# A gate bias matmul over 9 rows instead of 128, and four setup steps of VectorE in another order

## The chip, the core and the metric

The program runs on one core of a Trainium2 chip. A core has TensorE (PE: matmuls, with the weight load PEld as a row of its own), VectorE (DVE), ScalarE (ACT), GpSimd (POOL) and SyncE (SP), whose queue starts DMAs. Each engine runs its own list of instructions in order, and the lists meet only at semaphores: an instruction counts one up, another engine waits for a count. The metric is the device time in microseconds (us) of one execution, the median of three runs.

## The reference

Four layers on an activation of shape (16, 512, 256), each followed by a layer norm; cut to what is computed:

```python
x = layernorm(x + attention(x))            # 16 query heads, one key/value head of 16
x = layernorm(x + ternary_ffn(x))          # weights round(w/mean|w|) clipped to -1, 0, 1; gelu
x = layernorm(x + ssm_and_cfc(x))
x = layernorm(x + mx_quantised_linear(x))  # FP6 blocks of 32

def ssm_and_cfc(x):                        # S = 512 time steps, in order
    xn = layernorm(x) * norm_g + norm_b
    B_all = xn @ B_w.T + B_b
    states = A_pow * cumsum(B_all / max(A_pow, 1e-8))
    ssm_out = states @ C_w.T + C_b
    def step(h, xt):
        cat = [xt, h]
        ff1 = tanh(cat @ ff1_w.T + ff1_b); ff2 = tanh(cat @ ff2_w.T + ff2_b)
        t = sigmoid((cat @ ta_w.T + ta_b) * 0.1 + (cat @ tb_w.T + tb_b))
        return ff1 * (1 - t) + t * ff2
    return x + scan(step, ssm_out) @ out_w.T + out_b
```

The input-side biases of the three gates (`ff1`, `ff2`, `t`) are one number for each of 128 hidden units and each gate. The kernel adds them with a matmul, and that matmul is the one that changes.

## The kernel before, in words

The work is cut into 64 tiles of 128 rows (4 batch items by 32 positions). A tile passes through stages that run in different turns of one loop (`tile_time`, 16 ticks of 4 slots a turn): queries, row maxima of the scores, attention, feed-forward, state scan, 8 recurrence steps, last layer. The tables `PE_AT`, `ACT_AT`, `DVE_AT` and `POOL_AT` say at which slot of a turn each engine does its part, so the order on each engine is fixed by hand. After the loop a tail does the recurrence steps that are left.

**The bias matmul.** `input_bias` (L740) opens the sum in PSUM for the 8 recurrence steps of a tile: 384 columns (8 steps, 3 gates, 16 batch items). Its stationary operand `bias_rows` has 9 meaningful rows, three bf16 pieces for each of three gates; its moving operand `gate_of` has ones in the row of its own gate. In the kernel before both have 128 partitions, the other 119 filled with zeros, which GpSimd writes (L1484 to L1493). In the loop it is issued once a turn at slot 4 (`INPUT=4`), between a score matmul (L698) and the six matmuls of the gates' state part (L746); in the tail five times more.

**The array's tiles.** A matmul is built with a part of the 128 by 128 array that it uses. L698, L740 and L746 use all of it. L730, L762 and L619 use 128 rows by 32 columns, four such beside one another. L560 and L562 use 64 rows by 128 columns each, and run as a pair.

**The setup.** Before the loop all engines run steps `b` = 0 to 18 that turn weights, make keys and values, and from `b` = 11 on take the row maxima of tile 0. PE issues a pair of score matmuls (`max_pair`, L560 and L562); DVE reduces it (`take_maxima`, L1122); PE waits for each reduction (`max_taken`) before the next pair. Between them DVE has `setup_part(b)`: at `b` = 11 the scale of the second ternary weight (L1157 to L1159), for which GpSimd waits to compare the weight with it (L1517), at 12 the ternary weight (L1162), which waits for GpSimd, at 14 the additions of the biases (L1190, L1191), which wait for PE's products with vectors (L665, L668, at `b` = 13). At 15 `order_queries` copies tile 1's queries (L1136, L1138). At `b` = 12 and 16 DVE also splits keys (`split_keys`, L1219 to L1225), ahead of all this.

Of the kernel before, what the change touches and what calls it, by code (L numbers as in the profile page):

```python
# [8 lines left out]
ACT = mybir.ActivationFunctionType  # L9
AX_X = mybir.AxisListType.X  # L10
F32 = mybir.dt.float32
BF16 = mybir.dt.bfloat16
FP8 = mybir.dt.float8e4

P = 128
BLOCK_POS = 32
GROUP = P // BLOCK_POS
TICKS = 16
SLOTS = 4 * TICKS
STEPS = 8  # L20
# [22 lines left out]
def block_net(nc, x, w_q, w_k, w_v, w_out, softmax_scale, W1, b1, W2, b2, A_log, B_w, B_b, C_w, C_b,  # L43
              norm_g, norm_b, ff1_w, ff1_b, ff2_w, ff2_b, ta_w, ta_b, tb_w, tb_b, out_w, out_b,
              ffn_w, ffn_bias, q_dram, m_dram, x2_dram, out):
    B, S, D = x.shape
# [56 lines left out]
    def wait(eng, sem, count):  # L103

        if count > 0:
            eng.wait_ge(sem, count)

    def settle(eng):

        eng.sem_inc(settled[eng.engine], 1)

    with ExitStack() as ctx:
        def sb(name, shape, dt=F32):
            return ctx.enter_context(nc.sbuf_tensor(name, shape, dt))

        def sem(name):
            return ctx.enter_context(nc.semaphore(name))

        def bank(name):  # L120
            return ctx.enter_context(nc.psum_tensor(name, [P, 512], F32))
# [6 lines left out]
        gate_bank = bank("gate_bank")  # L128
# [29 lines left out]
        bias_piece = sb("bias_piece", [P, 3, 3])  # L158
        bias_rest = sb("bias_rest", [P, 2, 3])
        bias_bf = sb("bias_bf", [P, 2, 3], BF16)  # L160
        bias_rows = sb("bias_rows", [P, P], BF16)
        gate_ones = sb("gate_ones", [P, STEPS, 3, B])
        gate_of = sb("gate_of", [P, STEPS, 3, B], BF16)
        apow = sb("apow", [P, S])
        ainv = sb("ainv", [P, S])
        small = sb("small", [P, 32])
# [86 lines left out]
        gate_made = sem("gate_made")  # L253
# [10 lines left out]
        bias_rows_made = sem("bias_rows_made")  # L264
# [114 lines left out]
        FIRST_MAX = 11  # L379
# [166 lines left out]
        def _(pe):  # L546
# [137 lines left out]
                max_pair(0, pair)  # L684
            pe.wait_ge(v_kept, R)
            pe.wait_ge(bias_rows_made, 1)
            pe.wait_ge(gate_made, 5)

            def tile_time(c, r, n):
                for t in range(TICKS):  # L690
# [236 lines left out]
        def _(act):  # L927
# [14 lines left out]
            def copy_x(m):  # L942
                act.wait_ge(filled[1], use(1, "XT", m) + 1)
                if m > 0:
                    act.wait_ge(filled[1], use(1, "Q", m - 1) + 1)
                act.activation(xTq[:, :, :], gen_bank[1][:, 0:D].rearrange("p (k t) -> p k t", k=KT), ACT.Copy).then_inc(emptied[1], 1)

            def first_piece(m):
                act.wait_ge(filled[1], use(1, "Q", m) + 1)
                wait(act, q_placed, 144 * m)  # L950
                act.activation(qpiece[:, 0, :, :], gen_bank[1][:, 0:D].rearrange("p (k t) -> p k t", k=KT), ACT.Copy).then_inc(q_hi, 1)  # L951

            def keep_keys(i):

                act.wait_ge(k_made, GROUP * (i + 1))
                wait(act, v_turned, i)
                wait(act, k_step, 3 * i - 1)
                act.activation(kvT[:, :], score_bank[0][:, :], ACT.Copy).then_inc(kv_kept, 1)

            def keep_values(i):  # L960
                act.wait_ge(v_turned, i + 1)
                act.wait_ge(ones_set, 1)
                act.activation(vaug[:, GROUP * i:GROUP * (i + 1), :, :].rearrange("p u t c -> p (u t) c")[:, :, 0:DK],
                               score_bank[1][:, :].rearrange("p (x c) -> p x c", c=2 * DK)[:, :, DK:2 * DK], ACT.Copy).then_inc(v_kept, 1)

            def copy_keys_x(b):
                act.wait_ge(xk_turned, b + 1)
                wait(act, k_made, b - 1)
                for k in range(KT):
                    act.activation(xTk[:, b % 2, k, :], gen_bank[k][:, :], ACT.Copy).then_inc(xk_copied, 1)  # L970
# [6 lines left out]
            def copy_group(i):  # L977
                for at, j in enumerate(group(i)):
                    copy_turned(i, at, j)
# [13 lines left out]
            for b in range(B + MORE):  # L993
                if b + 1 < B:
                    copy_keys_x(b + 1)
                if b < B and b % GROUP == GROUP - 1:
                    keep_keys(b // GROUP)
                if b % GROUP == 2 and b > GROUP:
                    keep_values(b // GROUP - 1)
                copy_group(2 + b)  # L1000
                if b == SECOND:
                    copy_x(1)
                if b == SECOND + 1:
                    first_piece(1)
                if b == SECOND + 2:
                    copy_x(2)
                if b == 15:
                    act.wait_ge(product, 1)
                    act.activation(gcT[:, :, :], gate_bank[:, 0:3 * P].rearrange("p (g n) -> p g n", g=3), ACT.Copy).then_inc(product_out, 1)
                if b == 17:  # L1010
                    act.wait_ge(bias_turned, 1)
                    act.wait_ge(gate_made, 5)
                    act.activation(bias_rows[0:9, :], gate_bank[0:9, 0:P], ACT.Copy).then_inc(bias_rows_made, 1)

            def tile_time(c, r, n):
                g0, g1 = gen_bank
# [81 lines left out]
        def _(dve):  # L1098
            made = [0]

            def link(ins):

                made[0] += 1
                ins.then_inc(setup_dve, 1)
                dve.wait_ge(setup_dve, made[0])
# [11 lines left out]
            def take_maxima(m, pair):  # L1117

                um, i = divmod(pair, 2)
                at = 4 * um + i  # L1120
                dve.wait_ge(max_scores, TICKS // 2 * m + pair + 1)
                dve.tensor_reduce(nmax[:, m % 2, at:at + 3:2], max_banks[:, :, :], AX_X, ALU.max, negate=True).then_inc(max_taken, 1)  # L1122

            def rest_piece(m):
                dve.wait_ge(q_hi, m + 1)
                dve.tensor_tensor(qrest[:, :, :].rearrange("p k t -> p (k t)"), gen_bank[1][:, 0:D],  # L1126
                                  qpiece[:, 0, :, :].rearrange("p k t -> p (k t)"), ALU.subtract).then_inc(emptied[1], 1)

            def order_queries(m):

                dve.wait_ge(q_placed, 144 * (m + 1))
                wait(dve, scores_ready, TICKS * (m - R + 1))
                settle(dve)
                wait(dve, max_scores, TICKS // 2 * (m - 1))
                settle(dve)
                dve.tensor_copy(qlow[HALF:P, m % 2, :, :, :].rearrange("p u h s -> p h u s"),  # L1136
                                lowstage[HALF:P, H // 2:H, :].rearrange("p h (u s) -> p h u s", u=GROUP)).then_inc(q_ordered, 1)
                dve.tensor_copy(qaug[0:SPLIT, m % R, :, :, :].rearrange("p u h s -> p h u s"),  # L1138
                                qstage[:, :, :].rearrange("p h (u s) -> p h u s", u=GROUP)).then_inc(q_ordered, 1)
# [5 lines left out]
            def setup_part(b):  # L1145
# [34 lines left out]
                if b == 8:  # L1180
# [2 lines left out]
                    link(dve.tensor_tensor(wfb, fq[:, :].rearrange("p (j i) -> p j i", i=QBLOCK),  # L1183
                                           fs[:, 2, :].unsqueeze(2).to_broadcast([P, nblk, QBLOCK]), ALU.mult))
                    assert made[0] == F_QUANTISED
                if b == 14:

                    dve.wait_ge(bias_sums, 1)
                    dve.wait_ge(setup_pool, 3)
                    link(dve.tensor_tensor(bias_b[:, :], gate_bank[:, 0:1], cols[:, C_BB:C_BB + 1], ALU.add))  # L1190
                    link(dve.tensor_tensor(bias_g[:, 0:3], gate_bank[:, 1:4], cols[:, C_G:C_G + 3], ALU.add))  # L1191
                    assert made[0] == BIASES_ADDED
# [21 lines left out]
            def split_keys(i):  # L1214

                dve.wait_ge(kv_kept, i + 1)
                wait(dve, k_written, 16 * i)
                settle(dve)
                dve.tensor_copy(kpiece[:, 0, :], kvT[:, :]).then_inc(k_step, 1)  # L1219
                dve.wait_ge(k_step, 3 * i + 1)  # L1220
                dve.tensor_tensor(kres[:, :], kvT[:, :], kpiece[:, 0, :], ALU.subtract).then_inc(k_step, 1)
                dve.wait_ge(k_step, 3 * i + 2)
                dve.tensor_copy(kpiece[:, 1, :], kres[:, :]).then_inc(k_step, 1)
                dve.wait_ge(k_step, 3 * i + 3)
                dve.tensor_tensor(kpiece[:, 2, :], kres[:, :], kpiece[:, 1, :], ALU.subtract).then_inc(k_split, 1)  # L1225

            for b in range(B + MORE):
                if b % GROUP == 0 and b > 0:
                    split_keys(b // GROUP - 1)
                if b == SECOND + 1:  # L1230
                    rest_piece(1)
                if b in range(FIRST_MAX, FIRST_MAX + TICKS // 2):
                    take_maxima(0, b - FIRST_MAX)
                setup_part(b)
                if b in (7, 15):
                    order_queries((b - 7) // 8)
            for pair in range(B + MORE - FIRST_MAX, TICKS // 2):
                take_maxima(0, pair)
            dve.wait_ge(decay_step, DECAY_STEPS + 1)
# [234 lines left out]
        def _(pool):  # L1474
# [15 lines left out]
                               pattern=[[0, STEPS], [3, 3], [0, B]], channel_multiplier=-1).then_inc(gate_made, 1)  # L1490
            pool.wait_ge(gate_made, 3)
            pool.tensor_copy(gate_of[:, :, :, :], gate_ones[:, :, :, :]).then_inc(gate_made, 1)
            pool.memset(bias_rows[:, :], 0.0).then_inc(gate_made, 1)  # L1493

            pool.wait_ge(gate_made, 5)

            def more_pieces(m):

# [224 lines left out]
```

## Time and profile before

| | |
|---|---|
| runs | 1884.25, 1884.9, 1890.87 us; median 1884.9 |
| profiled execution | 1890.87 us, of which the span from first to last instruction is 1888.9 us |
| PE busy | 1742.5 us, 92% of the span |
| DVE, ACT, POOL busy | 74%, 62%, 54% |
| mean granted TensorE clock | 0.973 |

The span has three parts: the setup up to about 93 us, the loop to about 1800 us, and the tail. Times in a timeline are counted from the start of the span. "Idle before" in a row is how long the engine stood before this instruction, and after the arrow stands what released it. The start of one matmul to the start of the next is what it costs on PE; the duration printed for one is longer, since matmuls overlap. The chain of waits shows each piece with what it adds to the end, so a matmul stands there with its spacing.

### The profile page before, as it was taken

What the parts mean: (1) busy time and instruction counts of PE and PEld (TensorE: products, weight loads), DVE (VectorE), ACT (ScalarE), POOL (GpSimd) and SP (SyncE); (2) the same over time, 40 slices, a digit from 0 to 9 for tenths busy, and PEclk for the clock granted to TensorE, in tenths of its full rate; (3) what the DMA queues carried; (4) which work ended last, traced back from release to release, by engine and by line L of the source; (5) the groups of instructions that cost most, each with busy time, mean ns of one, the idle gap of its engine ahead of it and who ended that gap; (6) DMA issues with size and microseconds to landing.
All of it is one profiled execution on the core that took longest, in us unless ns stands there. A gap on an engine that the chain in (4) does not pass through costs nothing.

```text
span 1888.9 us, 74578 instructions
## 1 busy us (share of the span) xinstructions
PE 1742.5 (92%) x29935; PEld 1278.7 (68%) x29935; DVE 1401.6 (74%) x2995; ACT 1172.5 (62%) x2795; POOL 1015.0 (54%) x3194
## 2 busy tenths in 40 slices
PE   6689999999999999999999999999999999999874
PEld 4446676777777767777677777777777777766653
DVE  4667778777877787778777887778777877787455
ACT  3356666666666666666666666666666666666521
POOL 4212255655565556555655565656555666556632
PEclk8899999999999999999999999999999999999965
DMA  9511111111111111111111111111111111111000
GB/s 243 133 39 42 42 37 51 45 44 38 50 45 44 41 48 46 43 41 47 48 41 42 46 50 39 45 44 50 39 45 42 51 43 45 39 48 29 20 21 21
DMA packets 140912, 92.94 MB, mean 49 GB/s; under 512 B 20196, under 2 KB 139800, under 8 KB 140568
## 3 DMA queue, kind: packets, MB, share of 16 engines
q1 hardware_dynamic: 136368, 87.91, 17.3%
q8 instruction: 237, 3.88, 0.9%
q10 hardware_dynamic: 4200, 0.27, 0.2%
q14 instruction: 107, 0.88, 0.1%
HBM read 31.50 MB, written 18.35 MB: 26 GB/s over the span
## 4 chain that ended last, share of the span: by engine, by line
PE 67%; DVE 9%; POOL 7%; issue 5%; DMA 5%; ACT 4%; SPq 2%; DVEq 0%; POOLq 0%; ACTq 0%
PE gen_bank L767 12%; PE value_bank L730 10%; PE score_bank L698 8%; PE gen_bank L869 6%; PE max_banks L560 6%; DMA qaug<-nmT 3%; PE gen_bank L808 3%; PE gen_bank L582 3%; PE gate_bank L762 3%; PE gen_bank L777 3%; DVE nmax L1122 3%; PE gen_bank L836 3%; ACT probs L1069 2%; PE gate_bank L746 2%; POOL total L1667 2%
## 5 line engine op out<-in xcount | busy, mean ns | idle before, releaser
L1069 ACT ACTIVATE probs<-score_bank 128x512 f32<-128x512 f32 x1024 | 588.9, 597 | 253.2 <-PE score_bank L698 248.5
L1122 DVE TENSOR_REDUCE nmax<-max_banks 128x2 f32<-128x1024 f32 x512 | 622.4, 1216 | 111.3 <-PE max_banks L562 102.5
L698 PE MATMUL score_bank<-qaug,kaug 98*128 98x512 bf16 x1024 | 361.7, 384 | 16.5 <-DMA qaug<-nmT 14.6
L730 PE MATMUL value_bank<-probs,vaug 128*32 128x128 f32 x8192 | 330.3, 279 | 0.0
L730 PEld LDWEIGHTS value_bank<-probs,vaug 128*32 128x32 f32 x8192 | 192.6, 109 | 124.1 <-issue 91.3
L767 PE MATMUL gen_bank<-w2T,hT 128*128 128x256 f32 x1024 | 258.4, 386 | 0.0
L1666 POOL TENSOR_TENSOR diff<-gates 128x16 f32<-128x16 f32 x472 | 106.1, 225 | 273.4 <-ACT gates L1075 272.2
L560 PE MATMUL max_banks<-kaug,qaug 64*128 64x512 bf16 x512 | 198.4, 388 | 54.3 <-DVE nmax L1122 53.7
L767 PEld LDWEIGHTS gen_bank<-w2T,hT 128*128 128x128 f32 x1024 | 184.7, 190 | 32.7 <-issue 13.8
L562 PE MATMUL max_banks<-kaug,qlow 64*128 64x512 bf16 x512 | 199.4, 389 | 0.0
L869 PE MATMUL gen_bank<-x1piece,w1Tb 128*128 128x128 bf16 x3072 | 194.9, 220 | 0.5 <-DVE x1rest L1397 0.5
L869 PEld LDWEIGHTS gen_bank<-x1piece,w1Tb 128*128 128x128 bf16 x3072 | 178.7, 98 | 21.8 <-issue 13.8
L1061 ACT ACTIVATE hT<-gen_bank,cols 128x128 f32<-128x128 f32 x512 | 146.4, 369 | 67.1 <-PE gen_bank L869 66.4
L762 PEld LDWEIGHTS gate_bank<-hseq,ghT 128*32 128x32 f32 x11328 | 167.7, 112 | 8.9 <-POOL hseq L1671 5.4
L698 PEld LDWEIGHTS score_bank<-qaug,kaug 98*128 98x128 bf16 x1024 | 94.2, 97 | 116.0 <-issue 45.9
L762 PE MATMUL gate_bank<-hseq,ghT 128*32 128x16 f32 x11328 | 169.4, 182 | 3.3 <-POOL hseq L1671 3.3
L1126 DVE TENSOR_TENSOR qrest<-gen_bank,qpiece 128x256 f32<-128x256 f32 x64 | 27.2, 425 | 177.1 <-ACT qpiece L951 177.1
L1588 POOL TENSOR_TENSOR qin<-x,qscale 128x256 f32<-128x256 f32 x64 | 39.6, 619 | 217.6 <-issue 213.8
L1667 POOL TENSOR_TENSOR total<-gates 128x16 f32<-128x16 f32 x472 | 146.7, 311 | 0.0
L1075 ACT ACTIVATE gates<-gate_bank 128x48 f32<-128x48 f32 x472 | 100.7, 213 | 62.4 <-PE gate_bank L762 58.9
L1671 POOL TENSOR_TENSOR hseq<-total,mixed 128x16 f32<-128x16 f32 x472 | 105.2, 223 | 36.9
L1553 POOL TENSOR_TENSOR rstd<-veps,neg_half 128x1 f32<-128x1 f32 x192 | 112.0, 583 | 16.1 <-POOL veps L1551 0.2
(233 smaller groups left out, 3014.4 us busy)
## 6 DMA issues: line engine op xcount, KB each, us to landing
qstage<-qpiece SPq DMA_DIRECT2D x384, 64.0 KB
lowstage<-qpiece SPq DMA_DIRECT2D x192, 64.0 KB
xt<-in_L_attn_x SPq DMA_DIRECT2D x64, 128.0 KB
xk<-in_L_attn_x SPq DMA_DIRECT2D x16, 512.0 KB, 7.5
residual<-x2s SPq DMA_DIRECT2D x64, 128.0 KB
x2f<-residual SPq DMA_DIRECT2D x64, 128.0 KB
out<-x SPq DMA_DIRECT2D x64, 128.0 KB
raw<-in_L_ffn_W SPq DMA_DIRECT2D x2, 1024.0 KB, 12.3
```

Source lines behind the costliest of these rows:

```text
L560: pe.matmul(max_bank[0][:, :], qaug[0:HALF, m % R, um, 4 * i:4 * i + 4, :].rearrange("p h s -> p (h s)"), kaug[0:HALF, m % R, :, um, :], s ...
L562: pe.matmul(max_bank[1][:, :], qlow[HALF:P, m % 2, um, 4 * i:4 * i + 4, :].rearrange("p h s -> p (h s)"), kaug[HALF:P, m % R, :, um, :], s ...
L698: pe.matmul(score_bank[t % 2][:, :], kaug[0:AUG, r, tt, u, :], qaug[:, r, u, :, :].rearrange("p h s -> p (h s)"), start=True, stop=True).t ...
L730: last = pe.matmul(value_bank[32 * g:32 * g + 32, :].rearrange("p (k t) -> p k t", k=HG)[:, :, uv * BLOCK_POS:(uv + 1) * BLOCK_POS], vaug[ ...
L762: last = pe.matmul(bank[q:q + 32, k * GW + g * B:k * GW + (g + 1) * B], ghT[:, g, q:q + 32], prev, start=False, stop=True, tile_position=( ...
L767: return pe.matmul(gen_bank[0][:, 0:D], hT[:, f, :], w2T[:, f, :], start=(f == 0), stop=(f == FT - 1), skip_group_check=True)
L869: last = pe.matmul(gen_bank[half][:, f * P:(f + 1) * P], w1Tb[:, k, (4 * half + f) * P:(4 * half + f + 1) * P], x1piece[:, piece, k, :], s ...
L1061: last = act.activation(hT[:, ft, :], gen_bank[half][:, f * P:(f + 1) * P], ACT.Gelu, bias=cols[:, C_B1 + ft:C_B1 + ft + 1])
L1069: act.activation(probs[:, t % 4, :], score_bank[t % 2][:, :], ACT.Exp).then_inc(exp_done, 1)
L1122: dve.tensor_reduce(nmax[:, m % 2, at:at + 3:2], max_banks[:, :, :], AX_X, ALU.max, negate=True).then_inc(max_taken, 1)
L1553: pool.tensor_tensor(rstd[:, i:i + 1], veps[:, i:i + 1], neg_half[:, :], ALU.pow).then_inc(ln_rstd[i], 1)
L1667: pool.tensor_tensor(total[:, :], gates[:, B:2 * B], gates[:, 0:B], ALU.add).then_inc(mix_step, 1)
```

## The change

`bias_rows`, `gate_ones` and `gate_of` get 9 partitions, so that the bias matmul contracts over 9 rows instead of 128. The zero fill of `bias_rows` goes, and with it a wait of ACT for GpSimd; the other waits for that step count to 4 instead of 5. In the setup, DVE adds the biases at `b` = 13 instead of 14, and does `setup_part` and `order_queries` of a step before `take_maxima` of that step instead of after it.

```diff
-        bias_rows = sb("bias_rows", [P, P], BF16)
-        gate_ones = sb("gate_ones", [P, STEPS, 3, B])
-        gate_of = sb("gate_of", [P, STEPS, 3, B], BF16)
+        bias_rows = sb("bias_rows", [9, P], BF16)
+        gate_ones = sb("gate_ones", [9, STEPS, 3, B])
+        gate_of = sb("gate_of", [9, STEPS, 3, B], BF16)
...
-            pe.wait_ge(gate_made, 5)
+            pe.wait_ge(gate_made, 4)
...
-                    act.wait_ge(gate_made, 5)
-                    act.activation(bias_rows[0:9, :], gate_bank[0:9, 0:P], ACT.Copy).then_inc(bias_rows_made, 1)
+                    act.activation(bias_rows[:, :], gate_bank[0:9, 0:P], ACT.Copy).then_inc(bias_rows_made, 1)
...
-                if b == 14:
+                if b == 13:
 
                     dve.wait_ge(bias_sums, 1)
                     dve.wait_ge(setup_pool, 3)
...
-                if b in range(FIRST_MAX, FIRST_MAX + TICKS // 2):
-                    take_maxima(0, b - FIRST_MAX)
                 setup_part(b)
                 if b in (7, 15):
                     order_queries((b - 7) // 8)
+                if b in range(FIRST_MAX, FIRST_MAX + TICKS // 2):
+                    take_maxima(0, b - FIRST_MAX)
...
-            pool.memset(bias_rows[:, :], 0.0).then_inc(gate_made, 1)
-
-            pool.wait_ge(gate_made, 5)
+
+            pool.wait_ge(gate_made, 4)
```

On DVE, at `b` = 11, before the change (L1157 to L1159 make the scale, L1122 reduces the first pair, L1219 begins the split of keys):

```order
L1154 TENSOR_REDUCE small<-raw 128x1 [waits loaded_w2,setup_dve]
L1122 TENSOR_REDUCE nmax<-max_banks 128x2 [waits max_scores,setup_dve]
L1157 TENSOR_SCALAR small<-gate_bank 128x1 [waits scale_sum]
L1158 TENSOR_SCALAR small<-small 128x1 [waits setup_dve]
L1159 TENSOR_SCALAR small<-small 128x1 [waits setup_dve]
```

And after it, where line numbers from here on are lower by one:

```order
L1153 TENSOR_REDUCE small<-raw 128x1 [waits loaded_w2,setup_dve]
L1156 TENSOR_SCALAR small<-gate_bank 128x1 [waits scale_sum,setup_dve]
L1157 TENSOR_SCALAR small<-small 128x1 [waits setup_dve]
L1158 TENSOR_SCALAR small<-small 128x1 [waits setup_dve]
L1121 TENSOR_REDUCE nmax<-max_banks 128x2 [waits max_scores,setup_dve]
```

The three scale instructions now stand ahead of the reduction. Further on DVE, `b` = 12 to 15, before (the reductions are those of pairs 2 to 5):

```order
L1122 TENSOR_REDUCE nmax<-max_banks 128x2 [waits max_scores]
L1162 SCALAR_TENSOR_TENSOR raw<-raw,small,probs 128x2048 [waits tern_made]
L1122 TENSOR_REDUCE nmax<-max_banks 128x2 [waits max_scores,setup_dve]
L1122 TENSOR_REDUCE nmax<-max_banks 128x2 [waits max_scores]
L1190 TENSOR_TENSOR bias_b<-gate_bank,cols 128x1 [waits setup_pool,bias_sums]
L1191 TENSOR_TENSOR bias_g<-gate_bank,cols 128x3 [waits setup_dve]
L1122 TENSOR_REDUCE nmax<-max_banks 128x2 [waits max_scores,setup_dve]
L1136 COPY qlow<-lowstage 64x8x4x32 [waits q_placed]
L1138 COPY qaug<-qstage 96x16x4x32
```

And after:

```order
L1161 SCALAR_TENSOR_TENSOR raw<-raw,small,probs 128x2048 [waits tern_made]
L1121 TENSOR_REDUCE nmax<-max_banks 128x2 [waits max_scores,setup_dve]
L1189 TENSOR_TENSOR bias_b<-gate_bank,cols 128x1 [waits setup_pool,bias_sums]
L1190 TENSOR_TENSOR bias_g<-gate_bank,cols 128x3 [waits setup_dve]
L1121 TENSOR_REDUCE nmax<-max_banks 128x2 [waits max_scores,setup_dve]
L1121 TENSOR_REDUCE nmax<-max_banks 128x2 [waits max_scores]
L1135 COPY qlow<-lowstage 64x8x4x32 [waits q_placed]
L1137 COPY qaug<-qstage 96x16x4x32
L1121 TENSOR_REDUCE nmax<-max_banks 128x2 [waits max_scores]
```

The ternary weight stands ahead of pair 2's reduction, the bias additions ahead of pair 3's, and the query copies ahead of pair 5's.

## Rows read from the trace of the kernel before

**Rows 1.** Page, chain that ended last, by engine and by line:

```profile
PE 67%; DVE 9%; POOL 7%; issue 5%; DMA 5%; ACT 4%; SPq 2%; DVEq 0%; POOLq 0%; ACTq 0%
PE gen_bank L767 12%; PE value_bank L730 10%; PE score_bank L698 8%; PE gen_bank L869 6%; PE max_banks L560 6%; DMA qaug<-nmT 3%; PE gen_bank L808 3%; PE gen_bank L582 3%; PE gate_bank L762 3%; PE gen_bank L777 3%; DVE nmax L1122 3%; PE gen_bank L836 3%; ACT probs L1069 2%; PE gate_bank L746 2%; POOL total L1667 2%
```

**Rows 2.** Instructions of line L740: duration min/median/max in ns, first and last start:

```profile
L740 PE MATMUL gate_bank<-gate_of,bias_rows x59: 323/327/328, 228.9 to 1779.2; 128*128 128x384 bf16 x59
...
L740 PE MATMUL max_banks<-gate_of,bias_rows x5: 326/527/527, 1800.3 to 1848.6; 128*128 128x384 bf16 x5
```

**Rows 3.** Chain of waits, 1000 to 1045 us: start, what it adds, piece:

```profile
1002.48 0.22 PE score_bank L698
...
1005.75 0.27 PE score_bank L698
1006.18 0.67 PE gate_bank L746 x6
...
1007.59 0.32 PE max_banks L560
```

**Rows 4.** Timeline of PE, 57.9 to 60 us: start, duration, line, shapes:

```profile
57.93 0.66 PE L592 MATMUL value_bank<-ident,raw_g 128*128 128x128 f32 x4
58.52 0.39 PE L560 MATMUL max_banks<-kaug,qaug 64*128 64x512 bf16 x1
...
58.84 1.09 PE L607 MATMUL gen_bank<-ident,xk 128*128 128x128 f32 x8
```

**Rows 5.** Timeline of PE, 3 to 6.6 us, matmuls over 16 rows:

```profile
5.29 0.39 PE L592 MATMUL score_bank<-ident,raw_kv 16*128 16x16 f32 x2
5.62 0.69 PE L592 MATMUL score_bank<-ident,raw_q 128*128 128x128 f32 x2
```

**Rows 6.** Timeline of DVE in the setup:

```profile
59.03 1.23 DVE L1122 TENSOR_REDUCE nmax<-max_banks 128x2 f32<-128x1024 f32 x1 [4.11 <-PE max_banks L562]
...
61.33 4.01 DVE L1221 TENSOR_TENSOR hT<-hT,kpiece 128x512 f32<-128x512 f32 x1
...
68.58 2.34 DVE L1162 SCALAR_TENSOR_TENSOR raw<-raw,small,probs 128x2048 f32<-128x2048 f32 x1
...
76.58 1.23 DVE L1122 TENSOR_REDUCE nmax<-max_banks 128x2 f32<-128x1024 f32 x1 [4.40 <-PE max_banks L562]
...
78.36 1.23 DVE L1122 TENSOR_REDUCE nmax<-max_banks 128x2 f32<-128x1024 f32 x1 [0.30 <-PE max_banks L562]
79.61 0.42 DVE L1136 COPY qlow<-lowstage 64x1024 bf16<-64x1024 bf16 x1
80.07 0.77 DVE L1138 COPY qaug<-qstage 96x2048 bf16<-96x2048 bf16 x1
...
81.41 0.69 DVE L1221 TENSOR_TENSOR hT<-hT,kpiece 128x512 f32<-128x512 f32 x1
...
83.20 1.22 DVE L1122 TENSOR_REDUCE nmax<-max_banks 128x2 f32<-128x1024 f32 x1
```

**Rows 7.** Timeline of POOL, the comparison of the second ternary weight:

```profile
60.80 5.72 POOL L1517 TENSOR_SCALAR probs<-raw,small 128x2048 f32<-128x2048 f32 x1 [8.75 <-DVE small L1159]
```

**Rows 8.** Timeline of PE in the setup, 65 to 94 us:

```profile
65.58 0.27 PE L592 MATMUL value_bank<-ident,raw_f 128*128 128x128 f32 x1
68.72 0.43 PE L560 MATMUL max_banks<-kaug,qaug 64*128 64x512 bf16 x1 [2.87 <-DVE nmax L1122]
...
69.96 2.70 PE L668 MATMUL gate_bank<-cols,gxT 128*128 128x1 f32 x12
72.52 1.95 PE L607 MATMUL gen_bank<-ident,xk 128*128 128x128 f32 x8
...
76.14 0.39 PE L560 MATMUL max_banks<-kaug,qaug 64*128 64x512 bf16 x1
...
93.27 0.61 PE L698 MATMUL score_bank<-qaug,kaug 98*128 98x512 bf16 x1 [0.42 <-DMA qaug<-nmT]
```

**Rows 9.** Busy time by engine, 69 to 70 us; third number from the end is PEclk:

```profile
69.00:70.00 1.00, 1.00 (x7) 0.92 (x5) 1.00 (x1) 0.00 (x0) 0.00 (x0) 0.50 0.94 189
```

## The prediction

> **What bounds the kernel now.** I read the page first, then the chain of waits, the instructions of L740, and the timelines of the setup, because the change touches two places only: one matmul in each turn of the loop, and the order of DVE between about 55 and 85 us. TensorE carries 67% of the chain that ended last [rows 1]. In the loop the chain runs through PE from one matmul to the next, and the bias matmul lies on it: between the start of the score matmul L698 and that of L746 there are 0.43 us, of which L698 takes 0.27 in the chain and the bias matmul the other 0.16 [rows 3]. 0.16 us is what 384 columns need at 2.4 GHz. L740 is issued 59 times in the loop and five times in the tail [rows 2]; from the first to the last of the 59 it is 1550.3 us for 58 turns, so a turn lasts 26.73 us. The chain gives 2% of 1888.9 us to L746, the next instruction after L740 [rows 1]; at 0.67 us each that is some 56 passes, so nearly every turn goes through here. A delay at this point is therefore paid in full in every turn, and a gain too.
>
> In the setup the reader is to see PE and DVE waiting for each other. DVE stood 4.11 us before the first reduction and 4.40 us before the fourth [rows 6]; PE stood 2.87 us before the third pair of score matmuls, until DVE had reduced the second [rows 8].
>
> **Nine rows instead of 128.** The columns stay 384, so the matmul itself still costs 0.16 us. What changes is its tile: 32 rows by 128 columns, between two matmuls that use the whole array. The trace has no such matmul in the loop, but it has the pair L560 and L562, with 64 rows each.
>
> *On leaving.* L698 and L560 both stream 512 columns. L698 adds 0.22 us to the chain, the pair L560 adds 0.32 [rows 3]: the following matmul on another form of tile starts 0.10 us later. The same in the setup, 58.52 to 58.84 [rows 4].
>
> *On entering.* Four L592 start at 57.93 and span 0.66; one lasts 0.27 [rows 4, 8], so the last started at 58.32, and L560 starts at 58.52, 0.20 us later. L607 has the same shape, and eight of it in 1.09 us [rows 4] are 0.12 us apart or a little less. Entering costs 0.08 to 0.09 us.
>
> With 32 rows the only case is in the setup, at the low clock: two L592 over 16 rows start at 5.29 and span 0.39, the next on the full array starts at 5.62 [rows 5]. If one lasts 0.27 here too, the second started at 5.41, 0.12 after the first, and the other form came 0.21 us after it: 0.09 for leaving. The switch price is there for this tile form too.
>
> I take 0.09 in and 0.10 out, 0.19 us a turn. The lower bound is 0, if the smaller tile causes no switch; the upper bound is 0.30, if this tile waits until the duration printed for L698 and L740 is over, which for L740 is 0.327 against the 0.16 it adds. Times 59: **+11.2 us** (0 to +17.7). In the tail most of the five already stand before a 32-column matmul, so one switch each is new, at the lower clock perhaps twice as dear (527 ns against 327 [rows 2]): +0.5 us (0 to +1).
>
> This is the place where two pages of the Trainium skill disagree about this change. "TensorE: Matmul & The Clock Gate", section on LDWEIGHTS, says that loading 32 rows takes as long as loading 128, since columns count. By that alone the edit costs nothing, and the sum would be that of the first rival below. "TensorEngine Tiling (Array Packing)", section Key Properties, says: "Changing tiling mode (not just tile) drains the TensorE". The trace agrees with the second where the tile form changes: 0.32 us against 0.22 for 512 columns [rows 3].
>
> **GpSimd.** It fills and masks the same 384 elements a partition, and one memset at about 5 us goes. It and ACT's dropped wait are far ahead of what uses them: no wait for them stands in the chain. 0 us; were a saving exposed, it would be the 0.2 us of a memset.
>
> **DVE's new order.** (1) L1157 to L1159 now stand ahead of the first reduction and fit in the 4.11 us for which DVE stood [rows 6]. So GpSimd's comparison, 5.72 us from 60.80 [rows 7], begins up to 4 us sooner and ends near 62.5 instead of 66.52. DVE's subtraction L1221 ran beside it and took 4.01 us; alone it takes 0.69 [rows 6]. It should end near 63.0 instead of 65.34. (2) The ternary weight, 2.34 us [rows 6], now stands ahead of pair 2's reduction. From 63.0: 1.1 for the rest of the split, 2.34, then 1.2 for the reduction, so it is done at about 67.6 and PE's third pair comes at 67.75 instead of 68.72: **-1.0 us**. If L1221 still takes its 4.01 us from 60.75, it is +0.7. (3) The bias additions wait for L668, which ends at 72.66 [rows 8], or 71.7 by the new clock of events, and hold back pair 3's reduction behind them until 73.2. PE needs it at the pair of 76.14 [rows 8], then 75.1. L607, L619 and L592 hide it, with 1.9 us to spare; if PE runs at 2.4 GHz here, with about 0.5. Queued behind this wait stand the reduction and after it the next ones, and nothing else. (4) The query copies, 1.2 us, come before pair 5's reduction, but the split of keys and the next reduction after it follow without the additions (0.3) and the gap of 0.30 [rows 6]: pair 6's, at 83.20, comes 0.6 us earlier. **-0.6 us**. From there to the first score matmul PE and DVE alternate, and all moves together. GpSimd's pieces of the biases begin five us earlier, but were not waited for.
>
> **The clock.** After having stood 2.87 us PE worked at a granted clock of 0.50, which is 1.2 GHz, at 69 us [rows 8, 9], and L607 still took 1.95 us at 72.52, against 1.09 at 2.4 GHz [rows 4, 8]. PE now stands 1.0 us less before it, so some of the work from 69 to 76 us may run at the higher clock: 0 to -3.5 us, half of it. I take -1.0, nearer to none.
>
> **Sum.** 11.2 + 0.5 - 1.0 - 0.6 - 1.0 = **+9.1 us**. The profiled execution took 1890.87 us, its span 1888.9 and 2.0 us around it; it would become 1900.0. It lies 6.0 us above the median of the runs, so the forecast for the median is 1884.9 + 9.1 = **1894.0 us**, +0.48%. What a measurement of this kernel can tell from no change is about 0.5%, 9.4 us: the forecast lies just inside.
>
> **The rivals.**
> *No switch price (not slower).* The full array keeps its weights and the 32-row tile is loaded beside them, while L698 streams for its 0.22 us. Place: L698 to L746, where 0.43 us stay 0.43. It decides if that stretch stays under 0.47. Then only the setup counts: 1884.9 - 2.6 = 1882.3 us. For it: none of the rows has this form in the loop. Against it: the pair of 64 rows pays.
> *Only one of the two switches shows.* The entry is hidden by L698's stream, the exit is not, as L746 needs all rows. 0.10 x 59 + 0.3 - 2.6 = +3.6: 1888.5 us. Against it: L592 to L560 shows the entry too.
> *A full drain.* 0.30 us a turn: 17.7 + 1 - 2.6 = +16.1, 1901.0 us. Against it: no switch in the rows costs over 0.10.
> *The new order starves PE.* The comparison still slows L1221, and the bias additions or copies hold a reduction that PE needs: +0.7 and no clock gain instead of -2.6. With the switches 1897.3 us. For it: 0.5 us to spare is little.
>
> **How the numbers follow.** Forecast 0.55, no switch price 0.19, one switch 0.10, full drain 0.08, starved setup 0.08. The forecast's own range is 1889 to 1899: 0.07 to 0.11 us per switch for two switches and 59 turns (8.3 to 13.0), and the clock's bounds. The range given, 1881 to 1899, takes in the rival without a price and leaves out the full drain and the edges of the others. Slower by over 0.5% (over 1894.3): 0.45 of the forecast, all of the drain and of the starved setup, 0.25 + 0.16 = 0.41. Faster by over 0.5% (under 1875.5) needs the case without a price, the whole clock gain and more: 0.02. The same: 0.57.
>
> **What the profile after would show.** If the switch price is right: L698 to L740 goes from about 0.22 to 0.31 us, L740 to L746 from 0.16 to 0.26, and a turn from 26.73 to 26.92 us, L740's duration unchanged. If the order is right: the comparison on GpSimd begins near 57 us, L1220 (L1221 before) is under 2.5 us, PE's third pair comes near 67.8, and the first L698 near 91 instead of 93.27. A turn that stays at 26.73 us makes the forecast wrong, and so does a turn over 26.98; a first L698 at 93 or later makes the setup part wrong.

## The result, and the profile after

| | before | after |
|---|---|---|
| median of 4 runs each, us | 1886.68 (1884.25 to 1890.87) | 1904.88 (1899.13 to 1907.02) |
| profiled execution / its span, us | 1890.87 / 1888.9 | 1905.95 / 1904.2 |
| granted clock, share of full | 0.973 | 0.969 |

The changed kernel is slower: ratio 1.009 [1.0059, 1.0119], +18.2 us. The forecast of +9.1 us had the right sign, half the size, and its range ended below the median.

The page after, busy times and the chain by engine:

```profile
PE 1766.7 (93%) x29935; PEld 1279.7 (67%) x29935; DVE 1399.6 (74%) x2995; ACT 1171.9 (62%) x2795; POOL 1014.8 (53%) x3193
...
PE 69%; DVE 8%; POOL 7%; issue 5%; DMA 4%; ACT 4%; SPq 2%; DVEq 0%; POOLq 0%; ACTq 0%
```

The chain leans on PE a little more than in [rows 1]. The instructions of L740 after (duration in ns min/median/max, first and last start):

```profile
L740 PEld LDWEIGHTS gate_bank<-gate_of,bias_rows x59: 90/91/91, 230.7 to 1792.1; 9*128 9x128 bf16 x59
L740 PE MATMUL gate_bank<-gate_of,bias_rows x59: 318/332/332, 230.7 to 1792.2; 9*128 9x384 bf16 x59
...
L740 PE MATMUL max_banks<-gate_of,bias_rows x5: 331/496/497, 1813.8 to 1862.8; 9*128 9x384 bf16 x5
```

L740 itself lasts 332 ns against 327 in [rows 2]: almost nothing shows in the instruction that was changed. What changed is when it and its neighbours start. The chain of waits after, one turn (start, what it adds, piece):

```profile
1011.05 0.22 PE score_bank L698
1011.27 0.27 PE gate_bank L740
1011.54 0.86 PE gate_bank L746 x6
1012.40 0.57 PE value_bank L730 x16
...
1013.15 0.32 PE max_banks L560
```

The same piece before, between those of [rows 3]:

```profile
1006.01 0.16 PE gate_bank L740
```

So the bias matmul adds 0.27 instead of 0.16, and the six state matmuls 0.86 instead of 0.67. The timeline of PE and of its weight loads (PEld) shows why. Before (start, duration, line, shapes):

```profile
1005.62 0.39 PE L698 MATMUL score_bank<-qaug,kaug 98*128 98x512 bf16 x1
1005.78 0.10 PEld L740 LDWEIGHTS gate_bank<-gate_of,bias_rows 128*128 128x128 bf16 x1
1005.85 0.33 PE L740 MATMUL gate_bank<-gate_of,bias_rows 128*128 128x384 bf16 x1
...
1006.02 0.83 PE L746 MATMUL gate_bank<-states,gcT 128*128 128x128 f32 x6
```

And after:

```profile
1010.89 0.38 PE L698 MATMUL score_bank<-qaug,kaug 98*128 98x512 bf16 x1
1011.20 0.09 PEld L740 LDWEIGHTS gate_bank<-gate_of,bias_rows 9*128 9x128 bf16 x1 [0.42 <-issue]
1011.20 0.33 PE L740 MATMUL gate_bank<-gate_of,bias_rows 9*128 9x384 bf16 x1
1011.46 0.52 PEld L746 LDWEIGHTS gate_bank<-states,gcT 128*128 128x128 f32 x4 [0.17 <-issue]
1011.47 0.94 PE L746 MATMUL gate_bank<-states,gcT 128*128 128x128 f32 x6
```

Before, L740's weights were loaded from 0.16 us after L698's start, 0.07 us ahead of their own matmul. After, the load starts 0.31 us after L698's start, together with its matmul. L698's 512 columns need 0.21 us at 2.4 GHz, so the load starts 0.10 us after they have gone in (the printed end of L698 is later, but ends of matmuls are modelled). The same goes for L746: over the 59 turns its first load starts 0.165 us ahead of the matmul in the median before, and with it after. Median spacings between starts, from the traces' instructions, 59 turns each:

| start to start, us | before | after | more |
|---|---|---|---|
| L698 to L740 (entering) | 0.226 | 0.322 | 0.096 |
| L740 to first L746 (leaving) | 0.166 | 0.262 | 0.096 |
| first to second L746 | 0.108 | 0.213 | 0.105 |
| last L746 to L730 | 0.205 | 0.205 | 0 |

So there are three delays of 0.10 us in a turn, where the prediction had two. The third stands one instruction behind the switch.

**The sum by profile.** The spans differ by 15.3 us: up to the first score matmul of the loop, 93.27 to 91.82 us, -1.45; from there to the first L740 +3.25; first to last L740 1550.3 to 1561.5, +11.2; the rest of the span +2.3. The third figure is smaller than 58 times 0.30 = 17.4 because this execution waited less often for the transfer of the maxima (waits of PE for it: us, times, longest; before, then after):

```profile
PE score_bank L698 <- DMA qaug<-nmT: 14.6, 18, 1.2
```

```profile
PE score_bank L698 <- DMA qaug<-nmT: 9.9, 15, 1.1
```

That accounts for 4.7 of the 6.2 us. The typical turn shows the change better than the mean: its median was 26.58 us before and 26.83 after, and the undisturbed one (tenth percentile) 26.52 and 26.82. The second figure, +3.25 us, comes mostly from the clock. In both executions PE stands some 1.9 us at about 126 us, waiting for DVE. Before, it goes on at the full clock; after, it works at half of it, 1.2 GHz, until about 133.5 us, and loses 2.9 us to the execution before in that stretch (the third number from the end is the granted clock; before, then after):

```profile
127.00:133.50 6.50, 5.02 (x71) 3.14 (x72) 5.56 (x10) 3.89 (x8) 0.73 (x1) 1.00 0.04 11
```

```profile
127.00:133.50 6.50, 6.11 (x45) 3.68 (x46) 4.54 (x9) 3.21 (x5) 0.72 (x1) 0.50 0.02 4
```

Such differences come and go between executions; the medians of the runs are the measure, and by them 17.7 us (59 x 0.30) of the 18.2 are the three delays.

**The setup after.** DVE:

```profile
56.90 0.15 DVE L1158 TENSOR_SCALAR small<-small 128x1 f32<-128x1 f32 x1
59.25 1.23 DVE L1121 TENSOR_REDUCE nmax<-max_banks 128x2 f32<-128x1024 f32 x1 [2.20 <-PE max_banks L562]
60.40 2.48 DVE L1218 CAST kpiece<-hT 128x512 bf16<-128x512 f32 x1
62.90 0.69 DVE L1220 TENSOR_TENSOR hT<-hT,kpiece 128x512 f32<-128x512 f32 x1
...
64.70 2.34 DVE L1161 SCALAR_TENSOR_TENSOR raw<-raw,small,probs 128x2048 f32<-128x2048 f32 x1
67.08 1.22 DVE L1121 TENSOR_REDUCE nmax<-max_banks 128x2 f32<-128x1024 f32 x1
72.19 0.16 DVE L1189 TENSOR_TENSOR bias_b<-gate_bank,cols 128x1 f32<-128x1 f32 x1 [3.88 <-PE gate_bank L668]
```

GpSimd and PE:

```profile
57.16 5.43 POOL L1515 TENSOR_SCALAR probs<-raw,small 128x2048 f32<-128x2048 f32 x1 [5.26 <-DVE small L1158]
```

```profile
68.36 0.39 PE L560 MATMUL max_banks<-kaug,qaug 64*128 64x512 bf16 x1 [2.83 <-DVE nmax L1121]
...
72.01 1.95 PE L607 MATMUL gen_bank<-ident,xk 128*128 128x128 f32 x8
...
91.82 0.61 PE L698 MATMUL score_bank<-qaug,kaug 98*128 98x512 bf16 x1 [0.42 <-DMA qaug<-nmT]
```

The comparison begins at 57.16 instead of 60.80 [rows 7] and the subtraction takes 0.69 us instead of 4.01 [rows 6]. What is slow beside the comparison now is the cast ahead of the subtraction, L1218, with 2.48 us against 0.36 to 0.43 elsewhere. PE still stood 2.83 us before the third pair, and L607 still took 1.95 us [rows 8].

### The profile page after: what moved, and what is told of

It reads as the page before. It is cut to its first block, busy times and chain, and to the rows that moved or that the text cites. A ratio compares the mean times of both kernels' runs of the same rounds, so it can differ in the third digit from the quotient of the medians.

```text
span 1904.2 us, 74576 instructions
## 1 busy us (share of the span) xinstructions
PE 1766.7 (93%) x29935; PEld 1279.7 (67%) x29935; DVE 1399.6 (74%) x2995; ACT 1171.9 (62%) x2795; POOL 1014.8 (53%) x3193
## 4 chain that ended last, share of the span: by engine, by line
PE 69%; DVE 8%; POOL 7%; issue 5%; DMA 4%; ACT 4%; SPq 2%; DVEq 0%; POOLq 0%; ACTq 0%
PE gen_bank L767 12%; PE value_bank L730 10%; PE score_bank L698 9%; PE gen_bank L869 7%; PE max_banks L560 6%; PE gen_bank L808 3%; PE gen_bank L582 3%; PE gen_bank L777 3%; PE gate_bank L762 3%; DMA qaug<-nmT 3%; PE gate_bank L746 3%; PE gen_bank L836 3%; ACT probs L1068 2%; DVE nmax L1121 2%; POOL total L1665 2%
## 5 line engine op out<-in xcount | busy, mean ns | idle before, releaser
L1121 DVE TENSOR_REDUCE nmax<-max_banks 128x2 f32<-128x1024 f32 x512 | 622.4, 1216 | 124.1 <-PE max_banks L562 115.2
L698 PE MATMUL score_bank<-qaug,kaug 98*128 98x512 bf16 x1024 | 362.9, 386 | 11.5 <-DMA qaug<-nmT 9.9
L730 PE MATMUL value_bank<-probs,vaug 128*32 128x128 f32 x8192 | 331.2, 280 | 0.0
L730 PEld LDWEIGHTS value_bank<-probs,vaug 128*32 128x32 f32 x8192 | 193.1, 109 | 125.0 <-issue 91.6
L767 PE MATMUL gen_bank<-w2T,hT 128*128 128x256 f32 x1024 | 258.4, 386 | 0.0
L767 PEld LDWEIGHTS gen_bank<-w2T,hT 128*128 128x128 f32 x1024 | 184.6, 190 | 32.7 <-issue 13.8
L869 PE MATMUL gen_bank<-x1piece,w1Tb 128*128 128x128 bf16 x3072 | 196.1, 221 | 0.5 <-DVE x1rest L1396 0.5
L869 PEld LDWEIGHTS gen_bank<-x1piece,w1Tb 128*128 128x128 bf16 x3072 | 179.9, 99 | 22.0 <-issue 14.1
L698 PEld LDWEIGHTS score_bank<-qaug,kaug 98*128 98x128 bf16 x1024 | 94.3, 97 | 111.6 <-issue 46.9
```

The source lines that it names most:

```text
L698: pe.matmul(score_bank[t % 2][:, :], kaug[0:AUG, r, tt, u, :], qaug[:, r, u, :, :].rearrange("p h s -> p (h s)"), start=True, stop=True).t ...
L730: last = pe.matmul(value_bank[32 * g:32 * g + 32, :].rearrange("p (k t) -> p k t", k=HG)[:, :, uv * BLOCK_POS:(uv + 1) * BLOCK_POS], vaug[ ...
L767: return pe.matmul(gen_bank[0][:, 0:D], hT[:, f, :], w2T[:, f, :], start=(f == 0), stop=(f == FT - 1), skip_group_check=True)
L869: last = pe.matmul(gen_bank[half][:, f * P:(f + 1) * P], w1Tb[:, k, (4 * half + f) * P:(4 * half + f + 1) * P], x1piece[:, piece, k, :], s ...
```

## The experiments

Each kernel is the kernel before with one edit, and was timed beside it on the same chip. "Turn" is the median distance from one bias matmul to the next in the profile, 26.58 us before (26.52 undisturbed); most kernels with a delay have less of the disturbance, so what a turn gained is taken from the spacings of its matmuls. The theory throughout is that each change of tile form makes the matmuls behind it late, that each turn pays it, and that DVE's order is worth little; the rivals change with the question.

**1. Nine rows alone** (`rows9_only`), all the rest as before.

```
-  pe.matmul(..., bias_rows[:, :], gate_of[:, :, :, :]...
+  pe.matmul(..., bias_rows[0:9, :], gate_of[0:9, :, :, :]...
```

> One edit to the kernel before: the bias matmul reads rows 0 to 9 of both operands, order of the setup unchanged. Theory (each change of the array's tile form delays the next matmul by 0.10 us, and the first matmul after it by 0.10 us more where it is fp32): L698 to L740 0.32 us, L740 to L746 0.26, first to second L746 0.21 instead of 0.11; median turn 26.83 us instead of 26.53; 11 to 19 us slower than before, a little more than the whole change, which has the better setup. Rival (the new order of the setup costs the time): no more than 2 us from before.

Measured 1906.41 against 1887.75, ratio 1.0098 [1.0073, 1.0122], +18.7 us; turn 26.82. The spacings are those of the table above (0.322, 0.262, 0.213). The chain in one turn:

```profile
1042.14 0.26 PE score_bank L698
1042.40 0.27 PE gate_bank L740
1042.67 0.87 PE gate_bank L746 x6
```

One line of the change gives the whole loss, and the rival (the new order of the setup costs the time, at most 2 us here) is out.

**2. DVE's order alone** (`order_only`), 128 rows.

```
-                if b == 14:
+                if b == 13:
...
-                if b in range(FIRST_MAX, FIRST_MAX + TICKS // 2):
-                    take_maxima(0, b - FIRST_MAX)
                 setup_part(b)
                 if b in (7, 15):
                     order_queries((b - 7) // 8)
+                if b in range(FIRST_MAX, FIRST_MAX + TICKS // 2):
+                    take_maxima(0, b - FIRST_MAX)
```

> Only the order of DVE in the setup is changed, the bias matmul keeps 128 rows. Theory: first L698 near 91.8 us, turns as before (median 26.53 us), 1.5 us faster, which the measurement can't tell from no change (0 to -3). Rival (the setup order costs the time): over 5 us slower.

Measured 1886.51, ratio 0.9992 [0.9978, 1.0006]; turn 26.58, first L698 at 91.12. A cost of the order above 1.1 us is excluded by the interval; a gain of 1 to 2 us can be neither shown nor excluded. The first L698 is no better evidence: in the nine profiles of kernels with the old order it lay between 90.54 and 94.01 us, so 91.12 and 91.82 are within what the old order gives too.

**3. 64 rows** (`rows64_only`) **and 4. 96 rows** (`rows96_only`): `[0:64]` and `[0:96]` in the same line. 64 rows still give a smaller tile, 96 do not.

> As rows9_only but with 64 rows, which is a tile of 64 by 128, another form than the whole array. Theory (change of form): the same three delays as with 9 rows, median turn 26.83 us, 11 to 19 us slower than before. Rival (the fewer the rows the slower the weight load or the matmul): less than half of the loss of 9 rows, median turn under 26.7.

> As rows9_only but with 96 rows, which still takes the whole array as its tile. Theory (change of form): no delay at all, L698 to L740 0.22 us, L740 to L746 0.16, median turn 26.53 us, within 2 us of before. Rival (any matmul of fewer than 128 rows pays): a median turn of 26.6 us or more, over 4 us slower.

Measured: 64 rows 1905.37, ratio 1.0096 [1.0073, 1.0118], turn 26.83; 96 rows 1887.46, ratio 1.0002 [0.9987, 1.0017], turn 26.53. The chain with 64 rows:

```profile
1039.67 0.27 PE gate_bank L740
1039.93 0.86 PE gate_bank L746 x6
```

With 96 rows:

```profile
1034.17 0.16 PE gate_bank L740
1034.33 0.67 PE gate_bank L746 x6
```

There is a step and no slope: 9 and 64 rows cost the same, 96 and 128 cost nothing. It is the form of the tile, not the number of rows.

**5. The bias last** (`bias_last9`): nine rows, the bias matmul after the six L746, so that it leaves to L730, whose tile has another form anyway. (Here each of the three gates opens its sum itself, and the gate sums are not those of the reference; the instructions are the same, in another order.)

```
-                input_bias(m, gate_bank)
+                input_waits(m, gate_bank)
                 for g in range(3):
-                    input_gate(m, gate_bank, g)
+                    input_gate(m, gate_bank, g, start=True)
+                bias_part(gate_bank, 0, STEPS, False)
```

> 9 rows, setup order of before; in the loop the bias matmul comes after the six state matmuls instead of ahead of them, so it stands before the 32-column matmuls L732, where the form changes anyway. Theory (0.10 us for each change of form, 0.10 more for an fp32 matmul that follows): one change more than before instead of two and the fp32 weight load, so +0.10 us a turn, median turn 26.63 us, 4 to 8 us slower than before. Rival (what costs is the 9-row matmul itself, wherever it stands): +0.30 us a turn as in rows9_only.

Measured 1894.71 against 1889.15, ratio 1.0038 [1.0025, 1.0052], +5.6 us; turn 26.67. The chain:

```profile
1035.41 0.71 PE gate_bank L753 x6
1036.12 0.26 PE gate_bank L742
1036.38 0.57 PE value_bank L730 x16
```

The last state matmul to the bias is 0.207 us (0.10 more than between two of them); the step into L730's form was paid before too (0.205). One delay of 0.10 is left of three, 5.9 us for 59 turns, as expected, and the rival (the nine-row matmul costs 0.30 wherever it stands) is out. The turn grew by 0.14 and not 0.10, though: the first two state matmuls, now right behind the score matmul and without a change of form, are 0.148 us apart instead of 0.108. This 0.04 was not expected.

**6. The bias ahead of the score matmul** (`bias_first9`): same code, but `input_bias` is called at the start of tick 1, so the matmul behind it is bf16.

```
+                    if t == 1 and live(n + LEAD["REC"]):
+                        input_bias(n + LEAD["REC"], gate_bank)
...
-                input_bias(m, gate_bank)
```

> 9 rows, setup order of before; in the loop the bias matmul comes just ahead of the score matmul of tick 1, so a bf16 matmul follows it and the fp32 state matmuls follow that. Theory: 0.10 us to enter, 0.10 to leave, and no 0.10 for fp32 weights, so +0.20 us a turn, median turn 26.73 us, 7 to 14 us slower than before. Rival (leaving costs 0.20 whatever follows): +0.30 us a turn, median 26.83.

Measured 1903.11, ratio 1.0081 [1.0064, 1.0097], +14.0 us; turn 26.82, and by the spacings +0.28 where +0.20 was expected. From bias to score matmul 0.250 (0.16 without a switch), from score to state matmul 0.226 and between the first two state matmuls 0.113: **with a bf16 matmul behind the switch the third delay is gone**. What was too much stood ahead of the bias: 0.442 us after the last L775, against 0.25 at this place before.

**7. The same place with 96 rows** (`bias_first96`), to price the place.

> bias_first9 with 96 rows instead of 9, so the place is the same and no form of tile changes. In bias_first9 the turn grew by 0.27 us where 0.20 was expected. If the place itself costs the 0.07 (its waits stand ahead of the score matmul): +0.07 us a turn, median turn 26.60 us, 3 to 6 us slower than before. If the missing 0.07 belongs to the change of form: median turn 26.53 us, within 2 us of before.

Measured 1893.57 against 1887.94, ratio 1.0035 [1.0023, 1.0047], +5.6 us; turn 26.70, and by the spacings +0.18. The 0.442 us are there with 96 rows too: the place costs 0.18, more than the 0.07 expected, and of the switch only the leaving showed on top of it in 6 (0.10 by the spacings; turns of 26.82 against 26.70). The whole runs give the place less, 5.6 us and at most 8.9, where 59 x 0.18 would be 10.6; where the rest went wasn't looked into. Entering was hidden where PE stood anyway. The weight loads show the leaving directly. With 96 rows:

```profile
1032.16 0.10 PEld L744 LDWEIGHTS gate_bank<-gate_of,bias_rows 96*128 96x128 bf16 x1 [0.44 <-issue]
1032.19 0.10 PEld L700 LDWEIGHTS score_bank<-qaug,kaug 98*128 98x128 bf16 x1
```

With nine:

```profile
1037.28 0.09 PEld L744 LDWEIGHTS gate_bank<-gate_of,bias_rows 9*128 9x128 bf16 x1 [0.44 <-issue]
1037.55 0.10 PEld L700 LDWEIGHTS score_bank<-qaug,kaug 98*128 98x128 bf16 x1 [0.19 <-issue]
```

The score matmul's weights come 0.03 us after those of the bias in the one case, beside the bias matmul, and 0.27 us after them in the other.

**8. Two halves, apart** (`halves9`): 192 columns ahead of the score matmul, 192 behind it, nine rows; twice the switches, the same columns. (The second half opens the sum anew, and the gate sums are not those of the reference.)

```
+            def first_half(m):
+                input_waits(m, gate_bank)
+                bias_part(gate_bank, 0, STEPS // 2, True)
...
-                input_bias(m, gate_bank)
+                bias_part(gate_bank, STEPS // 2, STEPS, True)
```

> 9 rows, setup order of before; the 384 columns are split into two matmuls of 192, one ahead of the score matmul of tick 1 and one behind it. The columns are the same, the changes of form are four instead of two. Theory: 0.10 + 0.10 + 0.10 + 0.20 = +0.50 us a turn, median turn 27.03 us, 22 to 31 us slower than before. Rival (a fixed price of the 9-row operand or of its 384 columns): +0.30 us a turn or less.

Measured 1920.23, ratio 1.0172 [1.0153, 1.0192], +31.1 us; turn 27.12, and by the spacings +0.58 (expected +0.50). With the place at 0.18, a leaving to bf16, an entering and a leaving to fp32 it is 0.18 + 0.10 + 0.10 + 0.20 = 0.58.

**9. Two halves, together** (`halves_together9`): the same two matmuls, one behind the other.

```
+                for k in (0, STEPS // 2) ...:
+                    pe.matmul(bank[:, k * GW:e * GW], bias_rows[0:9, :], gate_of[0:9, k:e, :, :]...
```

> rows9_only with the 384 columns in two matmuls of 192 that follow one another, both behind the score matmul of tick 1; as halves9 but without the two further changes of form. Theory (changes of form cost, matmuls of the same form don't): median turn 26.83 us or up to 0.03 more, 14 to 20 us slower than before. Rival (each 9-row matmul pays): near the 27.1 us of halves9.

Measured 1907.77 against 1887.94, ratio 1.0112 [1.0093, 1.0130], +19.8 us; turn 26.83, as with one matmul. The price is per change of form, not per matmul over few rows.

## Why the prediction was wrong

Right: the change acts at two places only; L740 is on the path in every turn; the smaller tile makes its neighbours late (the rival without a switch price would have needed L698 to L746 under 0.47 us, and it is 0.584); entering costs 0.10 (0.09 predicted); the matmul after it starts 0.10 us late (0.10 predicted); L740's duration hardly moves. GpSimd's and ACT's parts cost nothing: with them in, +18.2 us, and with the one line alone +18.7.

**The step that failed** is the one headed "On leaving": 0.10 us, read as "the following matmul on another form of tile starts 0.10 us later", and the switch term of 0.19 us a turn made from it. It priced the start of the matmul behind the switch and not the one behind that. In the turn leaving costs 0.10 and then 0.105 more, 0.30 in all, and 59 x 0.30 = 17.7 us took the place of 11.2. With it the prediction's own sum is 15.6 us and its median 1900.5, outside the range. The change measured is 9.1 us more than the forecast one: 6.5 are this term, and the other 2.6 have the size of what was counted on for setup and clock, of which no gain can be shown.

One sign came out by luck. The prediction wanted a turn of 26.92 us instead of 26.73, and the mean turn in this execution is 26.92. But it holds fewer waits for the transfer of the maxima than the 26.73 of before; in the turns without them the step is 26.52 to 26.82, 0.30 and not 0.19.

The missing piece stood in the trace of before, three instructions from the row that I used. Behind the 64-row pair the first two L767, fp32, start 0.320 us apart, the others 0.216. The timeline before has it (start and duration of the group, whole and cut after its first):

```profile
1007.85 0.48 PE L767 MATMUL gen_bank<-w2T,hT 128*128 128x256 f32 x1
...
1007.85 1.56 PE L767 MATMUL gen_bank<-w2T,hT 128*128 128x256 f32 x6
```

The first lasts 0.48 us, the later ones 0.38. The last of six starts at 1007.85 + 1.56 - 0.38 = 1009.03, so five distances make 1.18 us where 5 x 0.216 = 1.08 would do. I took the price from what the pair adds to the chain and let the group behind it pass as one row. The 32-row case of the setup was misread as well: by their own starts the two L592 are 0.129 us apart and the next comes 0.192 after the second, 0.06 for leaving and not 0.09.

Why it is 0.10 for bf16 and 0.20 for fp32: in both traces the load of L740's or L698's bf16 weights lasts 0.09 to 0.10 us and that of L746's fp32 ones 0.19, and these are what the switch exposes, since the load no longer lies beside the matmul before. That agrees with the kernels in which the next matmul's type differs (fp32 in 1, 3 and 9, bf16 in 6). The type alone doesn't set the price: the trace of before has three kinds of matmul behind the 64-row pair, 55 cases or more of each, and the first of each comes 0.10 us late. Then the second is later than its like by 0.010 us for the bf16 L869 (load 0.095), by 0.056 for the fp32 transposes L573 (load 0.138) and by 0.104 for the fp32 L767 (load 0.186). In all that is 0.11, 0.16 and 0.20 us, each 0.02 more than the load lasts. L607 in [rows 4] is of the middle kind; its first load and that of L767 (start, duration):

```profile
58.83 0.14 PEld L607 LDWEIGHTS gen_bank<-ident,xk 128*128 128x128 f32 x1 [0.23 <-DMA xk<-in_L_attn_x]
```

```profile
1007.84 0.19 PEld L767 LDWEIGHTS gen_bank<-w2T,hT 128*128 128x128 f32 x1 [0.23 <-issue]
```

In experiment 5, too, the fp32 matmul behind the switch, L730, has a short load (32 columns, 0.106 us), and leaving costs 0.10. So the price on leaving goes with the load of the weights behind the switch. Whether the array is also emptied, and holds the load back by that, no run shows. The Trainium skill says both: "TensorE: Matmul & The Clock Gate", section "The mechanism", says that a load is pulled ahead of a running matmul if its rows don't conflict or it goes to the background buffer, and "TensorEngine Tiling (Array Packing)", section Key Properties, that a change of mode drains TensorE. The traces agree with the first within one form (the load is 0.165 us ahead of L746), and are consistent with the second across forms (0.002). The rule on load time that the prediction weighed is borne out nearly, 91 ns for nine rows against 96 for 128, but it is beside the point: the time of a load matters once the load is exposed.

The rivals: "a full drain" had the right size, 0.30 us a turn and 1901.0 us, and eight per cent. I held against it that no switch in the rows costs over 0.10, which the L767 rows contradict. It took the size from L740's printed duration, though, and that mechanism isn't what the rows show: with 0.327 us until L746, the spacing L740 to L746 would be 0.33, and it is 0.26. Even so, its 1901.0 would have been near. "Only one of the two switches shows" came true in experiments 5 and 6, where one of them is covered, not here. "The new order starves PE" is out by experiment 2.

The setup: step (1) was right in the subtraction (0.69) and wrong in that nothing else would be slowed; the cast was slow instead. The third pair came at 68.36, 0.36 us sooner and not 1.0. The first L698 came 1.45 us sooner (1.6 predicted without the clock), but that lies within the spread of that start between executions. No clock gain appeared: after PE's stand the granted clock was 0.50 from 70 to 74 us in both profiles. All of this is small: the order, priced at -2.6 us with the clock, measured -1.2 in experiment 2, with an interval that takes in both zero and -2.6.

Still open: what sets when the transfer of the maxima lands late, which moves single executions by several us, and whether 59 x 0.30 leaves anything over; the four kernels with nine or 64 rows in the old place gave +17.6 to +19.8 us, so perhaps 1 us for the tail.

## What to carry to other kernels

Cutting a matmul's rows saves no time on TensorE if the columns stay, and below the size where the tile changes form (64 rows did, 96 did not) it costs in each pass, if its neighbours use the whole array: here 0.10 us to enter, and on leaving about what the next weights take to load, 0.11 to 0.20. If such a tile is needed, put it next to an instruction that changes form anyway, or where PE stands, and keep its matmuls together. When you price a disturbance from a trace, compare the next three or four instructions with their undisturbed like, not just the first; a grouped row hides the second.

## What was not expected of the hardware

- The third delay: an fp32 matmul behind a change of form is itself on time but for 0.10 us, and holds the next one for another 0.10 (0.213 us against 0.108); with a shorter fp32 load it is 0.06 (0.165 against 0.109, L573).
- A transpose of 16 columns over all 128 rows, L859, pays nothing in the loop: it comes 0.109 us after L777 and L698 0.109 us after it, as between two such transposes of 128 columns. Which tile it is built with isn't on record.
- Two places for one 96-row matmul differ by 0.17 us a turn with the array's form unchanged (the bias stands 0.442 us behind the last fp32 matmul there, the score matmul in its stead 0.25). The bias matmul brings a semaphore instruction of its own (0.051 us on PE's sequencer); in the old place it stands beside the score matmul, in the new one it starts 0.336 us behind the last L775, and the bias's load 0.076 us after it. That is where to look; no run tests it.
- Some vector instructions on DVE beside GpSimd's comparison over 2048 elements last several times their usual: 4.01 us (L1221, [rows 6]) or 2.48 (L1218), against 0.69 and 0.36 to 0.43. Not all do: the reduction L1121 beside it took its usual 1.23 us, and in the trace of before the same cast (L1219 there), begun 0.07 us after the comparison, took 0.43. What decides it is open.
